# Layer-0/layer-1 attention: SyncE waits for each transfer of a sample's body to land before it issues the next

## The reference

```
# layer 0: attention over channels; q, k from ctx (y), v from x
q, k, v = conv1x1(Wq, ctx), conv1x1(Wk, ctx), conv1x1(Wv, x)        # 8 heads of 32
attn = softmax(q @ k^T over positions / sqrt(256))                  # 32 x 32 per head
o = conv1x1(Wo, attn @ v) + x
x1 = group_norm(o over channels and positions) * gn_w + gn_b
# layer 1: attention in chunks of 64 positions; q, k, v all from ctx
u = (softmax(q @ k^T / sqrt(32), key mask) @ v) @ W_out^T + b_out
z = u * mask + x1
out = instance_norm(z over positions)
```

## Time and profile before

| | us |
|---|---|
| median of 3 runs (lowest, highest) | 1556.32 (1548.07, 1556.88) |
| the profiled execution's own time | 1561.99 |
| its span | 1560.2 |
| mean granted clock of TensorE in it | 0.981 |

### The profile page before, as it was taken

The page is one execution under the profiler, slowest core; times in us unless marked ns, Lnnn a source line. Parts: engine busy times, 40 slices in busy tenths (PEclk is TensorE's granted clock), DMA queues, the critical chain, the costliest instruction groups (busy, mean ns, idle before and its releaser), DMA issues.

```text
span 1560.2 us, 54661 instructions
## 1 busy us (share of the span) xinstructions
PE 1474.8 (95%) x24146; PEld 1249.3 (80%) x24146; DVE 1261.6 (81%) x1944; ACT 1127.7 (72%) x1966; POOL 433.9 (28%) x292
## 2 busy tenths in 40 slices
PE   8999999999999999999999999999999999999984
PEld 5788787887878888888788887888878888878863
DVE  4678877888878888988889787888978878788876
ACT  5668667686777877777687776877767777777864
POOL 1113224042240422324133240422324132240420
PEclk9999999999999999999999999999999999999997
DMA  5222232432324233232423324333232322324121
GB/s 217 79 89 84 83 116 70 144 93 73 115 71 147 91 101 114 81 128 79 141 85 98 101 83 130 96 102 111 84 122 83 129 96 85 117 78 142 35 78 60
DMA packets 96396, 157.28 MB, mean 101 GB/s; under 512 B 5408, under 2 KB 38304, under 8 KB 96032
## 3 DMA queue, kind: packets, MB, share of 16 engines
q1 hardware_dynamic: 96160, 153.78, 30.4%
HBM read 120.20 MB, written 33.55 MB: 99 GB/s over the span
## 4 chain that ended last, share of the span: by engine, by line
PE 90%; DVE 4%; issue 4%; ACT 1%; DMA 0%; POOL 0%; ACTq 0%; SPq 0%; POOLq 0%; DVEq 0%
PE pj_ps L312 45%; PE l_ps L312 12%; PE s_ps L341 7%; PE s_ps L327 6%; PE l_ps L422 6%; PE s_ps L355 5%; PE l_ps L439 2%; PE l_ps L466 2%; PE l_ps L460 1%; DVE yt_hl L882 1%; PE l_ps L469 1%; DVE row_sum L921 1%; DVE z_stats L1020 1%; ACT prob L659 0%; PE s_ps L497 0%
## 5 line engine op out<-in xcount | busy, mean ns | idle before, releaser
L1221 POOL TENSOR_TENSOR prob<-prob,row_inv 128x1024 f32<-128x1024 f32 x128 | 244.9, 1919 | 582.2 <-DVE row_inv L925 580.7
L312 PE MATMUL pj_ps<-y_hi,w_hi 128*128 128x512 f32 x510 | 218.3, 428 | 5.9 <-ACT q_s L637 4.5
L312 PE MATMUL pj_ps<-y_hi,w_lo 128*128 128x512 f32 x510 | 202.7, 398 | 1.8 <-issue 1.8
L312 PE MATMUL pj_ps<-y_lo,w_hi 128*128 128x512 f32 x510 | 202.7, 397 | 0.0
L1238 POOL TENSOR_TENSOR o_sb<-o_sb,u_sb 128x1024 f32<-128x1024 f32 x60 | 155.4, 2600 | 162.8 <-ACT o_sb L682 161.2
L908 DVE TENSOR_REDUCE row_max<-s_ps 128x16 f32<-128x1024 f32 x128 | 155.7, 1216 | 28.2 <-PE s_ps L327 27.9
L921 DVE TENSOR_REDUCE row_sum<-prob 128x16 f32<-128x1024 f32 x128 | 155.6, 1216 | 13.3 <-ACT prob L659 11.4
L915 DVE TENSOR_TENSOR prob<-s_ps,row_max 128x1024 f32<-128x1024 f32 x128 | 156.7, 1224 | 4.4
L648 ACT COPY v_s<-pj_ps 128x512 f32<-128x512 f32 x128 | 74.1, 579 | 118.6 <-PE pj_ps L312 118.6
L312 PE MATMUL pj_ps<-w_hi,y_hi 128*128 128x256 f32 x512 | 153.0, 299 | 3.9 <-issue 2.1
L653 ACT COPY prob_t<-s_ps 128x512 f32<-128x512 f32 x256 | 136.6, 590 | 19.6 <-PE s_ps L341 19.6
(11 more groups left out here) (137 smaller groups left out, 3520.9 us busy)
## 6 DMA issues: line engine op xcount, KB each, us to landing
y_raw<-in_ctx SPq DMA_DIRECT2D x64, 512.0 KB, 4.9
yt_raw<-in_ctx_t SPq DMA_DIRECT2D x64, 512.0 KB, 3.6
x_raw<-in_x SPq DMA_DIRECT2D x64, 512.0 KB, 4.0
out_z<-o_sb SPq DMA_DIRECT2D x60, 512.0 KB, 4.4
mask_b<-in_mask SPq DMA_DIRECT2D x64, 256.0 KB, 3.4
out_z<-o_sb SPq DMA_DIRECT2D x8, 256.0 KB, 2.7
u_sb<-in_w SPq DMA_DIRECT2D x2, 512.0 KB, 6.0
w_sb<-in_w SPq DMA_DIRECT2D x1, 1024.0 KB, 10.9
```

The lines of the kernel that those rows point to most:

```text
L312: last = mm(dst, lhs, rhs, start=i == 0, stop=i == len(todo) - 1)
L1221: nc.gpsimd.tensor_tensor(cut, cut, row_inv[:, b % 2, e, :].unsqueeze(2).to_broadcast([P, 2 * HEADS, CHUNK]), ALU.mult).then_inc(probs_don ...
```

## The change

A helper, `landed`, waits on the semaphore that a transfer raises as it lands, at the count that this transfer brings it to. It is called right behind each of the 20 transfers of a sample's body. What stands ahead of the first body and behind the last one is as before, and the programs of the other engines are too.

```diff
@@ -224,6 +224,10 @@
                     sp.wait_ge(yt_lo_done, count(n, 4, q - 2))
                 sp.dma_start(yt_raw[:, q % 2], yt_d[n + q // 4][:, (q % 4) * PAIRS:(q % 4 + 1) * PAIRS, :]).then_inc(yt_in[q % 2], 16)
 
+            def landed(sem_in, n, per, i):
+
+                sp.wait_ge(sem_in, count(n, per, i, 16))
+
             def load_x(n, q):
                 if exists(n, 4, q - 2):
                     sp.wait_ge(x_hi_done, count(n, 4, q - 2))
@@ -267,16 +271,20 @@
                     if j == 0:
                         if not (last and b + 3 >= BLOCKS):
                             load_y(n, b + 3)
+                            landed(y_in[(b + 3) % 2], n, 2, (b + 3) // 2)
                         if not (last and b + 2 >= BLOCKS):
                             load_mask_b(n, b + 2)
+                            landed(mask_b_in[(b + 2) % 4], n, 1, (b + 2) // 4)
                     if not first and s in T_STORE:
                         store(n - 1, T_STORE.index(s))
-                    for first_slot, load in ((S_GRAM[0], load_yt), (S_X, load_x)):
+                        landed(stored[T_STORE.index(s)], n, 1, -1)
+                    for first_slot, load, sem_in in ((S_GRAM[0], load_yt, yt_in), (S_X, load_x, x_in)):
                         q = s - first_slot + 2
                         if last and load == load_x:
                             q += 1
                         if 2 <= q < 6 and not (last and q >= 4):
                             load(n, q)
+                            landed(sem_in[q % 2], n, 2, q // 2)
 
             over_samples(sp, body)
 
```

## The result

The changed kernel takes 1545.95 us (median of 20 runs, 1537.54 to 1552.32) against 1554.59 us before (20 runs, 1548.07 to 1562.60). The ratio is 0.9941, with a 95% interval of 0.9924 to 0.9958: 0.6% or some 9 us **faster**. The profiled execution has a span of 1544.3 us, 15.9 us less than that of before, which was among the slower executions of its kernel.

What follows compares the result with a forecast made beforehand. PE, busy 95% of the 1560.2 us span, was taken as the bound. Loop 0 plus tail 1.4 gave +1.4 us, so 1557.7 us against the median of 1556.32; range 1546 to 1572.

Steps and rivals of the forecast that it cites:

- rival C: Small matmuls of L355: PE's instruction fetches find an emptier queue; 10 us gained, 1547 us; chance 0.07.
- all 18 pauses: PE's idle waits on "issue" ahead of the small matmuls of L355, 31.9 us in 18 waits.
- the trio: yt, y and mask issued together in every sample; pauses of about 1.4 us there might go, 10 us in seven samples.
- The rule on queues: Engines serve queues packet by packet, so an instruction fetch never stands behind all that is queued; gain near nothing.
- The loop term: Serial transfers in the loop, tight in slots 11 to 13: between 0 and 3 us a sample, taken as 0.
- The chain from x to store(1): Slots 11 to 13: x(2), y(6), mask(5), store(1) end to end, reckoned 14.7 us; PE stalls only above 15.7.
- rival B: `copy_output(n, 1)` in slot 13, then `copy_k` and v projection: late stores stall PE each sample; 1572 to near 1600 us; chance 0.13.
- The tail term: Last sample: first waiting store goes after x(3) lands, so lands 1.4 us later; cost 1.4 to 3.4, taken as 1.4.
- the paragraph on it: Tail: PE's longer idle time may drop the clock to 1.2 GHz; twelve matmuls would cost 2.4 us more; not counted.
- below, 0 (nothing waits for these landings now, so nothing is to be gained from earlier ones): Lower bound of the loop's cost: 0, so no gain from earlier landings.

Runs made afterwards that it cites:

- the one wait: Kernel before with only one landing wait per sample, behind the mask of slot 12: 1544.60 us, 0.9930 of the kernel before.
- the shifted pair: Kernel before, no landing waits, mask and store(1) of slot 12 held together until ACT copied the first half of layer 0's output: 1544.93 us, 0.9941.
- the added load: Kernel with one landing wait behind slot 12's mask, plus an unread 512 KB load right behind that mask: 1554.24 us, 0.9985 of the kernel before.

## Why the prediction was wrong

**The forecast of 1557.7 us** lay on the wrong side: the time is 1545.95, some 9 us under that of before. It fell out of the range by a hair at the low end (1546.0).

**The step that failed is the one that set rival C aside**: it was given 0.07, with the sentence that "the position of the block in the stream of short instructions seems to set it, not the load". That was read from one pause with a lone mask in flight, 2.02 us, no shorter than one with three transfers, 1.70. The two readings are both true of these two places: neither pause went away. The step from there to all 18 pauses was not. What was missed are the five places with a mask and a store in flight (761.96, 855.93 and so on in the trace of before). There the load decides, as the one wait, the shifted pair and the added load show, and 10 us lay there. That the position sets the others is not shown either. The size given to C, 10 us and 1547, was near the mark, and so was the row (issue ahead of L355 near 20, measured 20.0); its place, the trio, was wrong.

**The rule on queues** went the same way. The Trainium skill says (*DMA: Bandwidth & Descriptors*, section Queues, rings and completion order) that an engine goes round its queues packet by packet, from which I took that the gain would be near nothing. The runs speak against that as an account of this fetch: a mask and one 512 KB transfer queued ahead bring pauses of 1.4 to 2.6 us where there were none. They speak for it in that a second 512 KB adds next to nothing, and a lone mask or a lone store brings no pause at the five places.

**The loop term, 0, was nearly right.** The chain from x to store(1) was reckoned at 14.7 us; in the sample of the earlier trace rows it is 13.75 in the changed kernel (x issued at 465.60, store at 476.21 and landed 3.15 later, worked out from the trace), since the lone transfers took 3.7, 3.8, 3.1 and 3.2 us and not 3.9, 4.1, 3.1 and 3.3. The handing over cost nothing that shows. Its reader started 1.5 us behind the landing, where 0.33 had been reckoned with the old distance. But rival B, 0.13, did happen in three samples, at just the place it named. In sample 7 a store took 4.8 us to land instead of 3.3, so that the chain came to 16.1 us, over the 15.7 of the prediction:

```profile
759.24 1.27 ACT L715 ACTIVATE o_sb<-l_ps,o_bias 128x512 f32<-128x512 f32 x2 [1.72 <-DMA out_z<-o_sb]
```

```profile
762.08 0.39 PE L320 MATMUL pj_ps<-w_hi,y_hi 128*128 128x256 f32 x1 [0.92 <-ACT k_s L649]
```

All but 0.8 us of ACT's wait reaches PE, where 0.67 had been reckoned, and so at the other two. The loop cost PE 1.9 us in the first profile and 1.5, in two samples, in the second.

**The tail term was mis-sized**: +1.4 us forecast; the wait grew by 3.1 and PE's pause by 3.1, because the store took 5.3 us, and the clock dropped as the paragraph on it had feared. In the second profile of the changed kernel ACT's longest wait is 4.8 and PE's pause 2.3, so this is not what each execution pays.

**The sentence "below, 0 (nothing waits for these landings now, so nothing is to be gained from earlier ones)"** closed the sum to a gain. It is true of the readers of the data. It left out that the transfers share the DMA engines with a reader that appears in no wait as a DMA: PE's instruction stream.

## What to carry to other kernels

Where PE is at 95% and runs bursts of very short matmuls, look at each pause with the releaser "issue" of over a microsecond: ask when its block of instructions moved and what transfers had been queued ahead of it. Do not judge by one such pause; list them by their place in the matmul sequence and compare two traces place by place: here five hung on what was queued, and most of the others stayed when nothing overlapped any more. One wait that kept a large transfer out of the queue for some three microseconds, where its reader had that slack, brought as much as serialising everything, and did not lengthen the pause in the tail (1.21 us, against 1.56 and 1.17 in the two profiles of before).

## What was not expected of the hardware

Most pauses for instructions repeat at the same matmul from one execution to the next, some to the hundredth (1.80, 2.58 and 1.29 us in both profiles of before; others differ by up to 0.8 us, and some come and go), though executions differ by 14 us. At such a pause PE goes on 2.1 us or more after its block begins to move.

A block of instructions behind a mask of 256 KB and a transfer of 512 KB comes 1.9 to 3.5 us later in PE's work than in the changed kernel; behind a second 512 KB, not later still.

A store of 512 KB with nothing of SP's beside it takes 2.7 to 3.7 us in 49 of the 60 cases of the changed kernel and 4.1 to 5.3 in the other 11; why, was not tried.
